# Two token routings beside a light attention: where the iterations of the coordinate descent are placed in the engines' queues

## What is computed

```python
def _coor_descent(s, k):
    b = -s; cur = 4.0
    for _ in range(20):
        sb = (s + b) / cur
        a = cur * (logk - logsumexp(sb, axis=-1, keepdims=True))
        b = -relu(s + a)
        cur = max(cur * 0.7, 0.03)
    return exp((s + a + b) / cur)
```

## Time and profile before

| | |
|---|---|
| median of two runs | 8574.22 us (8554.24 and 8594.2) |
| the profiled execution | 8535.81 us |
| its span, slowest core (core 5) | 8534.3 us, mean granted TensorE clock 0.742 |
| busy: PE, DVE, ACT, POOL | 5564.8, 3271.3, 1411.5, 324.9 us |
| the stretch of p2b and b2 | 290.9 to 747.9 us |
| the stretch of c2 | 747.9 to 1631.2 us |
| the experts | 4042 to 8534.3 us |

### The profile page before, as it was taken

How to read it: one execution, slowest core, us unless ns; L and a number is a source line. 1 busy time by engine, 2 the same in 40 slices (tenths; PEclk the granted TensorE clock), 3 DMA queues, 4 the chain that set the end, 5 groups by cost and what they waited for, 6 DMA issues and landing times.

```text
span 8534.3 us, 71804 instructions; the slowest of 8 cores (8458.8 to 8534.3 us)
## 1 busy us (share of the span) xinstructions
PE 5564.8 (65%) x22320; PEld 2093.3 (25%) x22320; DVE 3271.3 (38%) x5992; ACT 1411.5 (17%) x1826; POOL 324.9 (4%) x337
## 2 busy tenths in 40 slices
PE   5124222255545555470898888988988889888897
PEld 1001000013333333210232332323323223233232
DVE  2753444474444444325232332333323333233232
ACT  1121000002222222211111111111111111111111
POOL 0131000000000000000000000000000000000000
PEclk8556555575555555585997999989989898799998
DMA  2101000110000000000211121221212121202110
GB/s 92 39 5 10 0 0 1 40 15 1 1 1 1 1 1 1 23 27 11 35 28 19 16 31 16 31 30 17 31 16 31 16 31 17 30 16 31 16 31 40
DMA packets 149718, 169.25 MB, mean 20 GB/s; under 512 B 56132, under 2 KB 125268, under 8 KB 142948
## 3 DMA queue, kind: packets, MB, share of 16 engines
q0 software_dynamic: 140688, 111.63, 9.3%
q1 hardware_dynamic: 8660, 53.04, 1.7%
HBM read 267.68 MB, written 8.39 MB: 32 GB/s over the span
## 4 chain that ended last, share of the span: by engine, by line
PE 44%; DVE 4%; issue 2%; ACT 1%; DMA 1%; POOL 0%; DVEq 0%; ACTq 0%; PEldq 0%; POOLq 0%
PE pSIM L1431 22%; PE pSIM L1505 13%; PE pSIM L1436 4%; PE pMISC L1392 2%; PE pMISC L1473 2%; DVE x L1528 1%; PE pSIM L1511 1%; ACT gtmp L1455 1%; DVE gTq L1466 1%; DVE gtmp L1460 1%; DMA b3ce<-b3c 1%; DVE u2sb L1484 0%; PE pSIM L1414 0%; DVE u3sb L1410 0%; DVE u1sb L1405 0%
## 5 line engine op out<-in xcount | busy, mean ns | idle before, releaser
L1505 PE MATMUL pSIM<-gTq,w2b 128*128 128x512 bf16 x4096 | 1229.8, 449 | 303.2 <-DVE gTq L1466 225.5
L1528 DVE SCALAR_TENSOR_TENSOR x<-pSIM,x 128x512 f32<-128x512 f32 x1024 | 708.2, 692 | 804.0 <-PE pSIM L1505 449.4
L1431 PE MATMUL pSIM<-xl2T,w1b 128*128 128x512 bf16 x4096 | 995.9, 387 | 22.0 <-DVE u3sb L1410 22.0
L1431 PE MATMUL pSIM<-xl2T,w3b 128*128 128x512 bf16 x4096 | 988.3, 385 | 0.0
L1460 DVE TENSOR_TENSOR gtmp<-gtmp,gtmp 128x512 bf16<-128x512 bf16 x512 | 217.7, 425 | 1885.9 <-ACT gtmp L1455 1885.9
L1446 ACT ACTIVATE gtmp<-pSIM,b1ce 128x512 bf16<-128x512 f32 x512 | 351.8, 687 | 2975.7 <-PE pSIM L1436 2946.8
L1505 PEld LDWEIGHTS pSIM<-gTq,w2b 128*128 128x128 bf16 x4096 | 388.7, 108 | 1056.4 <-issue 886.2
L1059 PE MATMUL pT<-idbf,attnbf 128*128 128x128 bf16 x2048 | 258.8, 306 | 589.6 <-ACT attnbf L1043 564.3
L1431 PEld LDWEIGHTS pSIM<-xl2T,w1b 128*128 128x128 bf16 x4096 | 363.1, 99 | 519.6 <-issue 187.9
L1431 PEld LDWEIGHTS pSIM<-xl2T,w3b 128*128 128x128 bf16 x4096 | 361.3, 98 | 490.4 <-issue 156.2
L1455 ACT ACTIVATE gtmp<-pSIM,b3ce 128x512 bf16<-128x512 f32 x512 | 351.7, 687 | 733.5 <-PE pSIM L1436 733.5
(11 more groups left out here) (267 smaller groups left out, 4850.9 us busy)
## 6 DMA issues: line engine op xcount, KB each, us to landing
w1b<-w1q POOLq DMA_DIRECT2D x32, 1024.0 KB, 11.6
w3b<-w3q POOLq DMA_DIRECT2D x32, 1024.0 KB, 15.9
w2b<-w2q POOLq DMA_DIRECT2D x32, 1024.0 KB, 19.0
xs<-xT SPq DMA_DIRECT2D x24, 1024.0 KB, 4.9
xc<-xT SPq DMA_DIRECT2D x16, 1024.0 KB, 5.1
out<-x SPq DMA_DIRECT2D x8, 1024.0 KB, 11.0
wst<-wqkv POOLq DMA_DIRECT2D x8, 256.0 KB, 4.4
cos<-cos SPq DMA_DIRECT2D x1, 1024.0 KB
```

Of the source, the lines that this page charges most:

```text
L1431: E.matmul(pSIM[:, 512 * bank:512 * bank + 512], wb[:, 512 * dc + 128 * hc:512 * dc + 128 * hc + 128], xl2T[:, 2048 * dc + 512 * tc: 2048 ...
L1505: ins = E.matmul(pch(yb), w2b[par][:, 1024 * hc + 128 * dc: 1024 * hc + 128 * dc + 128], gTq[:, 512 * hc:512 * hc + 512], start=(hc == 0), ...
L1528: E.scalar_tensor_tensor(x1[:, 2048 * dc + 512 * tc: 2048 * dc + 512 * tc + 512], pch(yb), 1.0, x1[:, 2048 * dc + 512 * tc: 2048 * dc + 51 ...
```

## The change

The feeding points of `c1s1` in p2b and b2 are gone. The same 181 instructions, with the same waits, are fed in c2 over its first 40 iterations. The feeding of `c1stage` starts after them and takes 80 iterations (40 to 119) instead of 110 (0 to 109). No instruction is added or removed.

```diff
-    c1pts = [0]
-
-    def feed1():
-        c1pts[0] += 1
-        P.feed(c1s1, c1pts[0] / 28.0)
 
     for dc in range(8):
         ...
-        feed1()
     P.flush("p2b")
...
              inc=S["vec2"], drain=True)
-        feed1()
     for fc in range(8):
...
-            if tc == 3:
-                feed1()
-    P.feed(c1s1, 1.0)
-    assert not any(c1s1[1].values())
-    PEND.clear()
     P.flush("b2")
...
-        P.feed(c1stage, (it + 1) / 110.0)
+        P.feed(c1s1, (it + 1) / 40.0)
+        P.feed(c1stage, (it - 39) / 80.0)
+    P.feed(c1s1, 1.0)
     P.feed(c1stage, 1.0)
+    assert not any(c1s1[1].values())
     assert not any(c1stage[1].values())
```

## The result

The changed kernel takes 0.9917 of the time of the kernel before, 95% interval 0.9886 to 0.9947. On 8574 us that is -71 us, -0.8%; the forecast was -70. The forecast time of 8504 us was built on 8574, the median of two runs; the ratio on the same base gives 8503. The medians of all runs of the two kernels are 8458.91 us (20 runs) and 8554.24 us (19 runs). The profiled execution of the changed kernel has a span of 8456.3 us against 8534.3.

What follows compares the result with a forecast made beforehand. The prediction held V to the descent's pace, p2b to DVE, c2 to its round trip. Its terms, -250 ahead of c2, +197 in c2, -17 ranking, gave -70 us: 8574 to 8504, range 8440 to 8580.

Steps and rivals of the forecast that it cites:

- first and second pattern: c2's first 40 iterations: two ways a nine-instruction round is cut over two iterations, adding 10.95 and 8.78 us a round.
- saved ahead of c2: p2b, V, Q and K: without the descent's pieces c2 begins at about 498 instead of 747.99; 250 us saved.
- the descent in c2: c2's first 40 iterations: 20 rounds in DVE's and ACT's queues add 197 us, between 100 and 304.
- hold of the scaling: c2: POOL's subtract holds DVE's scaling L831 until it ends; 2.93 us in ten rounds, 1.56 in ten.
- ranking: c2, `c1stage` fed denser: fewer iterations pay the comparisons' fixed tail; 17 us saved, between 0 and 30.
- What bounds it: V goes at the descent's pace, 15.20 us a round; p2b is bound by DVE, a bare c2 iteration by its 5.10 us chain.
- Rival B: c2: POOL's subtract does not hold the scaling L831; 45 us less, 8459 us; chance 0.15.
- Rival C: c2, iterations 0 to 39: nothing of the descent hides, 15.2 us a round, 304 instead of 197, 8611 us; chance 0.12.
- `wvfull`: Load issued beside the clearing: by the page V starts about 9 us later; the sum was left without it.
- D: V, Q and K: the projections' matmuls stay at 1.2 GHz; 81 us more, 8585 us; chance 0.08.
- E: Experts' part: the gain is real but lost in the clock granted to the slowest core; 8575 us; chance 0.15.
- behind it: Behind c2: no instruction moved, so the time there changes by no more than the cores' scatter.

Runs made afterwards that it cites:

- one_before: Kernel before with only the first of the descent's 20 rounds kept; ratio 0.9705 to the kernel before, first masking of c2 at 505.0 us, c2 879.9 us.
- one_after: Changed kernel with only the first of the descent's 20 rounds kept; ratio 0.970 to the kernel before, c2 868.9 us, 195.3 shorter than in the changed kernel.
- dve_sub: Changed kernel with the descent's 2x2048 subtract on DVE instead of POOL; ratio 0.991 to the kernel before, c2 3.5 us longer than in the changed kernel.
- spread60: Changed kernel with the descent fed over 60 iterations, the ranking over the next 60; ratio 0.9787 to the kernel before, c2 98.1 us shorter than in the changed kernel.
- dense20: Changed kernel with the descent fed over 20 iterations, the ranking over the next 100; c2 57.7 us longer than in the changed kernel.
- rank44: Changed kernel with the ranking fed over 44 iterations instead of 80; ratio 0.9897 to the kernel before, c2 19.8 us shorter than in the changed kernel.
- minform: Changed kernel, descent rewritten with min(s, -a), no subtract or relu, 19 rounds over 20 iterations, ranking over 44; ratio 0.9704 to the kernel before, c2 882.4 us.

## Why the prediction was right, point by point

| step | predicted | measured |
|---|---|---|
| p2b ends (last pass) | 384.7 | 383.17 + 1.35 = 384.5 |
| V starts | 402 | 403.4 |
| first Q matmul | 437 | 440.8 |
| c2 begins | 498 | 500.0 |
| pair of iterations, first and second pattern | 21.2, 19.0 | 21.18, 19.02 |
| saved ahead of c2 | 250 | 748.29 - 500.46 = 247.8 |
| the descent in c2 | 197 | 404.4 - 40 x 5.10 = 200.4 |
| hold of the scaling, part of it | 45 | 45.4 |
| ranking | -17 | -15 |
| at the start of d0a | -70 | 1570.24 - 1632.26 = -62.0 |
| behind it | 0 | 6886.1 - 6902.0 = -16 |

(404.4 us is from the first masking at 500.46 to the 41st, at 904.87. The ranking is what is left of c2: 1064.2 - 878.5 - 200.4 = -14.7.)

- *What bounds it.* That V and Q/K went at the pace of the descent was read from one coincidence, a 15.20 us round with a V tile in it. one_before shows it by taking the round away.
- *The saving* was 2 us too large. V tiles ran at about 2.0 instead of 1.9 us each, the 1.95 us between the two clearings stayed though I had put it down to nothing, and the first Q matmul came 4.9 us after the issue of its load instead of 4.6.
- *The descent in c2* was 3 us too small; both patterns are there, with the waits in the places named. Rival B fell in the profile: the subtract does hold the scaling. Rival C fell: 10.0, not 15.2 us a round. There is one table load in all of c2, as before.
- *The ranking* gained 15 instead of 17 us. The iterations that hold comparisons were 144.6 us longer in sum than 5.10 each before (74 iterations) and 130.9 after (55): 13.7 saved where 140 - 123 = 17 had been worked out, both sums being too small. Outside them the scaling beside the ranking's first POOL operation takes 4.70 us instead of 3.15, and the rest gains 2.6; why was not looked for.
- *What the prediction drew from the Trainium skill on `wvfull`* (page "SBUF — State Buffer"), a start of V 9 us later, did not come true: V started at 403.4. The issue, 0.91 us from 385.25, was over before the clearing began, and the load landed 10.1 us after it started. Nor does the clearing shut POOL out in the kernel before: beside L617 (452.30 to 459.61, its usual 7.31) POOL's subtract took its usual time,

```profile
455.97 4.48 POOL L556 TENSOR_TENSOR u_rt<-s_rt,rl_rt 2x2048 f32<-2x2048 f32 x1 [3.58 <-ACT rl_rt L580]
```

  so the prediction had put the page's sentence on an instruction that does not hold POOL up here. Whether a load's descriptors would wait for one that does, no run shows.
- *Rivals D and E.* The clock in V and Q/K went up, not down: D fell. E is the part that no step explains. Behind c2 no instruction moved, yet the profiled core needed 16 us less. The same stretch, on the slowest core of each profile but one_after's, took 6902.0 (before), 6886.1 (after), 6867.5 (one_before), 6861.9 (dve_sub), 6857.2 (spread60), 6856.0 (dense20), 6871.3 (rank44) and 6864.4 us (minform): a scatter of 46 us with no order by what was changed ahead of it. All eight cores of the two profiles settle it: each reached d0a 56 to 66 us earlier, 61 in the mean, and behind that the changes run from -34 to +30 us, with means of 6855.4 and 6853.5 us. So the gain is made ahead of d0a and is not lost behind it. The profiled -78 us of the slowest core are 62 of the change and 16 of this scatter.
- *What was luck.* The stage sum is -62, not -70: the three terms missed by 2, 3 and 2 us, all the same way, which is small but did not cancel. That the ratio gives -71, a microsecond from the forecast, is luck; its interval is 26 us each way.

## What to carry to other kernels

A serial side chain that is fed into in-order queues costs whatever its host waits for, so cost it at each host by what the host was doing meanwhile: a dense host (the passes of p2b and the projections, 1.8 us of matmuls a tile) paid 12.8 us a round, a host full of round trips 10.0. More than the host matters the cut: end a piece where the next instruction would have to wait, and let long operations of the second engine stand behind the host's own, so that they run in its shadow (10 us a round became 5.8 with no instruction changed). Best is to shorten the chain: the algebra that left two long operations a round out of five took out most of the cost, which is then under 2 us a round.

## What the runs showed of the hardware

- A bf16 scaling of 128x256 on DVE (0.29 us) that becomes ready while POOL works on 2x2048 elements ends 0.07 to 0.10 us after POOL, however long that is (0.45 to 6.04 us, in all 91 such cases of c2 in the nine traces), although it touches 128 partitions and POOL two. DVE's masking (one operand in PSUM), its reductions and its copies out of PSUM ran on beside POOL at their usual 0.42, 0.42 and 0.28 us. The Trainium skill, "SBUF — State Buffer", section "SBUF: two separate sides", tells it as an exclusive lock on a shared pair of ports; by that rule, the traces agree.
- It also goes the other way round, which was missed when the kernel before was read. In its p2b two POOL operations on one element a partition, 0.18 us when alone, ended 0.05 us after the DVE pass beside them:

```profile
317.15 2.29 DVE L596 TENSOR_TENSOR xlt<-xs,mB 128x2048 f32<-128x2048 f32 x1
...
317.60 1.89 POOL L573 TENSOR_TENSOR sc_rt<-sc_rt 2x1 f32<-2x1 f32 x1 [19.79 <-ACT sc_rt L571]
...
319.55 2.29 DVE L598 TENSOR_TENSOR xlt<-xlt,rB 128x2048 f32<-128x2048 f32 x1
319.68 2.21 POOL L577 TENSOR_SCALAR sc_rt<-sc_rt 2x1 f32<-2x1 f32 x1 [0.18 <-POOL sc_rt L573]
```

  Relu waited 4.64 us for them instead of 0.87: here a pass holds the chain, and in the earlier trace rows the chain a pass.
- On cores 6 and 7 of the changed kernel the granted clock in V was 0.80 and 0.81 beside 0.91 to 0.92 on the other six, in the same execution, although cores 4 and 5 belong to the same die.
- exp with the sum taken by ACT's accumulator costs one more ACT instruction of 0.18 us (2x2048, in minform), in place of a DVE reduction of 2.27 us.
- A 2x2048 minimum against a per-partition value takes DVE 1.27 us, the subtract of two 2x2048 rows 2.28 us and POOL 4.48 us.
